# Weight quantizer of a two-layer mixture kernel: the rounding constant from ScalarE's Square instead of VectorE's masked exponent

## The chip, the cores and the metric

The kernel runs on one core of a Trainium2 chip. The metric is the device time of one launch in microseconds, the median of three runs. A profile is one further execution of the same program; its times come from that execution.

## The reference

The reference is a two-layer transformer body on x of 4 x 512 tokens of width 512. Only the first two of its four sublayers matter here:

1. x = x + tanh(g) * E(layernorm(x)), where E is a three-matrix expert (Wg, Wu and Wd are all `ctx_2048[e]`), and a token's expert e of four follows from its id. Tokens are sorted by expert into 19 slots of 128 rows.
2. x = x + tanh(g) * FFN(layernorm(x)), a SiLU-gated feed-forward net with 2048 hidden units whose activations and weights are rounded block by block. For a weight w the rounding is:

```
amax  = max |w| over a block of 32
scale = 2 ** (floor(log2(amax)) - 2)
v     = w / scale
step  = 2 ** (max(floor(log2|v|), 0) - 1)
q     = clip(round_half_to_even(v / step) * step, -6, 6) * scale
```

Layer 1 (attention over ctx, then a routed mixture of 64 experts) follows in the same kernel and is not touched.

## The kernel before, in words

All stages are in one program with one hand-written instruction stream for each engine, joined by semaphores. Stage 1 (about 15 to 213 us of the profile) does sublayer 1 and, beside it, quantizes and transposes the weights of sublayer 2, which stage 2 needs complete.

Sublayer 1 runs over SLOTS = 19 slots j. For a slot, GpSimd (POOL) gathers 128 rows by an indirect DMA (`gather`, L585), VectorE (DVE) takes mean and variance (`measure`, L904 and L905), POOL turns them into a scale and a bias (`deviation`, L592 to L594), ScalarE (ACT) normalises (`normal_h`, L1632), TensorE (PE) transposes (`turn_h`, L1283), ACT copies out of PSUM (`ht`, L1637), PE multiplies by the expert's matrix (`z`, L1294), ACT takes SiLU (`silu`, L1642), DVE the product (`product`, L910), PE transposes it (`turn_a`, L1303), ACT copies (`at`, L1647), PE multiplies again (`y`, L1310), ACT scales and copies (`y`, L1652), and POOL adds the rows into x_sum in DRAM by an indirect DMA (`scatter`, L616).

The weights are 16 tiles n of 128 x 1536 (512 columns each of gate, up and down). For a tile, SP loads it (L488 to L490), DVE takes the maximum of each block of 32 (`top`, L865), and makes the block's power of two and its inverse (`scales`, L871 and L874), and POOL multiplies the tile by the inverse into wy (`normal`, L600). Then DVE rounds by adding and subtracting a large constant, in two functions:

- `push` (L876 to L885): masks the exponent bits out of wy's upper half (L880), makes of them the constant ws = max(., 1/4) * 1.5 * 2^22 in bf16 (L883), and adds: wu = ws + wy (L885).
- `pull` (L887 to L895): wc = wu - ws (L890), clamps to +-1.5 (L892), multiplies by the block's power of two into wq (L895).

PE transposes wq in twelve pieces (`turn_w`, L1320) and ACT copies them into the stationary weights (`weights`, L1659 to L1662).

The order of the work is written out by hand. Tiles are paired with slots by TILED: slots with j % 4 != 3 have a tile, so 15 tiles have a slot and tile 15 comes after the last slot (REST). In a slot with tile n the engines do, in this order:

- DVE: scales(n+1), top(n+2), measure(j+4), product(j+1), pull(n), push(n+1); push(0) stands ahead of the loop, before measure(3)
- POOL: normal(n+1), scatter(j-1), deviation(j+3), gather(j+5)
- PE: z(j+1), turn_a(j), turn_h(j+2), turn_w of slot j-1, y(j)
- ACT: silu(j+1), at(j), ht(j+2), weights of slot j-1, y(j), normal_h(j+3)

Ahead of the loop ACT does normal_h(0), ht(0), normal_h(1), issues four DMAs (L1674), then silu(0), ht(1), normal_h(2). Stage 2 begins with SP's loads of x_sum (L508), which wait for the last scatter, and DVE's `enter` (L948), which stands behind the last pull.

Of the kernel before, what the change touches and what calls it, by code (L numbers as in the profile page):

```python
# [8 lines left out]
BF16 = mybir.dt.bfloat16  # L9
# [8 lines left out]
P = 128  # L18
# [17 lines left out]
W_MAGIC = 1.5 * 2.0 ** 22  # L36
W_TOP = 1.5
W_LOW = 0.25
# [58 lines left out]
def build(nc, x, ids, ctx, g_xattn, g_ffn, w_gate, w_up, w_down, gamma, gate_w, bias,  # L97
# [9 lines left out]
    with ExitStack() as st:  # L107
# [52 lines left out]
        def bank(n, m=1):  # L160
# [18 lines left out]
        wmax_ready, wm_ready, winv_ready, wy_ready, we_ready, ws_ready, wu_ready, wc_ready, wtop_ready, wq_ready = (  # L179
            sem(n) for n in ("wmax_ready", "wm_ready", "winv_ready", "wy_ready", "we_ready", "ws_ready", "wu_ready",  # L180
# [13 lines left out]
        we_bits = arena(W3 // 2, I16)  # L194
        ws = arena(W3 // 2, BF16)
# [287 lines left out]
        with nc.Block() as block:  # L483
# [302 lines left out]
            def _(dve):  # L786
# [90 lines left out]
                def push(n):  # L877

                    dve.wait_ge(wy_ready, n + 1)
                    dve.tensor_scalar(we_bits, wy[:, n % 2, :].bitcast(I16)[:, 1::2], EXP_MASK16, None,  # L880
                                      ALU.bitwise_and).then_inc(we_ready, 1)
                    dve.wait_ge(we_ready, n + 1)
                    dve.tensor_scalar(ws, we_bits.bitcast(BF16), W_LOW, W_MAGIC, ALU.max, ALU.mult).then_inc(ws_ready, 1)  # L883
                    dve.wait_ge(ws_ready, n + 1)
                    dve.tensor_tensor(wu, ws, wy[:, n % 2, :], ALU.add).then_inc(wu_ready, 1)  # L885

                def pull(n):  # L887

                    dve.wait_ge(wu_ready, n + 1)
                    dve.tensor_tensor(wc[:, n % 2, :], wu, ws, ALU.subtract).then_inc(wc_ready, 1)  # L890
                    dve.wait_ge(wc_ready, n + 1)
                    dve.tensor_scalar(wc[:, n % 2, :], wc[:, n % 2, :], W_TOP, -W_TOP, ALU.min, ALU.max).then_inc(wtop_ready, 1)  # L892
                    dve.wait_ge(wtop_ready, n + 1)
                    need(dve, wq_turned, n - 1)
                    dve.tensor_tensor(twos(wq[:, n % 2, :]), twos(wc[:, n % 2, :]),  # L895
                                      wm[:, n % 4].unsqueeze(2).to_broadcast([P, NB3, BLK // 2, 2]), ALU.mult).then_inc(wq_ready, 1)
# [21 lines left out]
                push(0)  # L918
                measure(3)
                product(0)  # L920
                for j in range(SLOTS):
                    n = tile_at(j)
                    if j in TILED:
                        scales(n + 1)
                        if n + 2 < NT:
                            top(n + 2)
                    if j + 4 < SLOTS:
                        measure(j + 4)
                    if j + 1 < SLOTS:
                        product(j + 1)  # L930
                    if j in TILED:
                        pull(n)
                        push(n + 1)
                for n in REST:
                    if n + 1 < NT:
                        scales(n + 1)
                    if n + 2 < NT:
                        top(n + 2)
                    pull(n)
                    if n + 1 < NT:  # L940
                        push(n + 1)
# [680 lines left out]
            def _(act):  # L1622
# [30 lines left out]

                def weights(n):
# [4 lines left out]
                    act.activation(WGT[:, :, cols], src[:, 0], ACT.Copy)  # L1659
                    act.activation(WUT[:, :, cols], src[:, 1], ACT.Copy)  # L1660
                    r = n % 4
                    act.activation(WDT[:, 4 * (n // 4):4 * (n // 4) + 4, r * P:(r + 1) * P], src[:, 2], ACT.Copy).then_inc(wq_out, 1)  # L1662
# [14 lines left out]
                normal_h(2)  # L1677
                for j in range(SLOTS):
# [3 lines left out]
                    if j + 2 < SLOTS:  # L1682
                        ht(j + 2)
                    if j - 1 in TILED:
# [199 lines left out]
```

## Time and profile before

| | us |
|---|---|
| median of 3 runs | 1055.89 (1052.69 to 1056.42) |
| time of the profiled execution | 1055.53 |
| span of its profile | 1053.7 |
| PE busy | 960.7 (91%) |
| DVE busy | 656.9 (62%) |
| POOL busy | 638.7 (61%) |
| ACT busy | 398.9 (38%) |

The span runs from the first to the last instruction seen; the time of the execution holds another 1.8 us around it. Busy shares are means over stages with different limits. An engine's stream is in order, so an instruction that waits holds up all that stands behind it on its engine.

### The profile page before, as it was taken

To read this page: it belongs to the slowest core of one execution; us is meant where nothing else is said; L and a number is where in the kernel's file an instruction comes from. 1 tells how busy PE (TensorE), PEld (TensorE's weight loads), DVE (VectorE), ACT (ScalarE), POOL (GpSimd) and SP (SyncE) were. 2 spreads that over 40 slices of the span, in tenths; PEclk is the share of its full clock that TensorE was granted. 3 is DMA by queue.
4 is the path that set the end of the run, shared out by engine and by line. 5 is a ranking of instruction groups with operands and counts; after the bars stand their busy time and mean duration, and the time that the engine had idled before them with its cause. 6 is when DMAs were issued, how large, how long until landed. Compare 5 with 4: busy or idle time off the path is not lost.

```text
span 1053.7 us, 13591 instructions
## 1 busy us (share of the span) xinstructions
PE 960.7 (91%) x4380; PEld 470.5 (45%) x4402; DVE 656.9 (62%) x1208; ACT 398.9 (38%) x801; POOL 638.7 (61%) x562
## 2 busy tenths in 40 slices
PE   4989999659999999799999999999999999999993
PEld 3445554324444444344444445335555555555530
DVE  6679887968888887677777777981222222222221
ACT  4434445324444444466666665332111111111100
POOL 4497887548878887686767671245444554445431
PEclk9989999869999999999999999999999999999996
DMA  7755555240000000240000605078999999999949
GB/s 260 239 121 138 125 127 131 39 160 1 2 1 1 1 2 13 75 163 21 21 21 25 245 1 200 21 260 259 335 335 331 334 339 330 335 334 338 253 54 193
DMA packets 64147, 162.89 MB, mean 155 GB/s; under 512 B 9888, under 2 KB 10032, under 8 KB 63632
## 3 DMA queue, kind: packets, MB, share of 16 engines
q1 hardware_dynamic: 47488, 116.94, 31.9%
q0 software_dynamic: 16464, 40.91, 18.0%
q10 hardware_dynamic: 128, 4.19, 1.2%
q8 instruction: 37, 0.61, 0.2%
q14 instruction: 30, 0.25, 0.1%
HBM read 129.67 MB, written 39.67 MB: 161 GB/s over the span
## 4 chain that ended last, share of the span: by engine, by line
PE 55%; POOL 17%; DVE 14%; issue 8%; ACT 2%; DMA 1%; ACTq 0%; POOLq 0%; DVEq 0%
PE PS L1570 16%; PE PS L1589 8%; PE PS L1414 6%; PE PS L1391 6%; PE PS L1402 6%; POOL ARENA L657 6%; POOL ARENA L663 3%; PE PS L1559 3%; PE PS L364 3%; DVE ARENA L985 2%; POOL XNT L600 2%; DVE ARENA L890 2%; POOL ARENA L652 1%; PE PS L1310 1%; DVE ARENA L1194 1%
## 5 line engine op out<-in xcount | busy, mean ns | idle before, releaser
L707 POOL TENSOR_TENSOR ARENA<-ARENA 128x512 f32<-128x512 f32 x128 | 133.2, 1061 | 54.5 <-DVE ARENA L1020 54.4
L1356 PE MATMUL PS<-SLAB,ARENA 128*128 128x512 bf16 x501 | 119.4, 385 | 13.4 <-DVE ARENA L971 10.8
L753 POOL DMA_INDIRECT out<-ARENA,idx x32 | 45.9, 1436 | 125.3 <-DVE ARENA L1226 116.3
L1836 ACT ACTIVATE ARENA<-PS 96x192 f32<-96x192 f32 x64 | 20.9, 326 | 226.4 <-PE PS L1570 226.4
L1226 DVE COPY ARENA<-PS 96x512 f32<-96x512 f32 x64 | 41.1, 682 | 94.8 <-PE PS L1589 94.8
L1743 ACT ACTIVATE ARENA<-PS,ARENA 128x512 f32<-128x512 f32 x128 | 86.8, 683 | 24.4 <-DVE ARENA L1014 21.2
L1014 DVE TENSOR_REDUCE ARENA<-PS 128x2 f32<-128x1024 f32 x64 | 78.2, 1221 | 8.3 <-PE PS L1391 8.0
L1356 PEld LDWEIGHTS PS<-SLAB,ARENA 128*128 128x128 bf16 x512 | 48.8, 99 | 76.1 <-issue 23.1
L1570 PE MATMUL PS<-SLAB,ARENA 128*96 128x384 f32 x240 | 81.0, 490 | 0.0
L1402 PEld LDWEIGHTS PS<-ident,ARENA 128*128 128x128 f32 x512 | 54.8, 141 | 51.1 <-issue 35.0
L663 POOL TENSOR_TENSOR ARENA<-ARENA 128x1024 bf16<-128x1024 fp8e4 x32 | 61.1, 1909 | 24.3 <-DVE ARENA L985 24.3
L657 POOL TENSOR_TENSOR ARENA<-ARENA 128x1024 f32<-128x1024 f32 x32 | 62.8, 1962 | 21.5 <-DVE ARENA L980 21.5
L1709 ACT ACTIVATE ARENA<-PS 128x512 f32<-128x512 f32 x64 | 38.2, 597 | 99.1 <-PE PS L1356 99.0
L746 POOL DMA_INDIRECT ARENA<-rows,idx x64 | 60.0, 938 | 23.4 <-issue 11.6
L1294 PE MATMUL PS<-CT,ARENA 128*128 x152 | 70.8, 610 | 2.8 <-ACT ARENA L1637 2.8
L1391 PE MATMUL PS<-ARENA 64*128 64x512 f32 x256 | 72.5, 643 | 0.2 <-ACT ARENA L1743 0.2
L1310 PE MATMUL PS<-CT,XNT 128*128 x152 | 70.7, 608 | 2.2 <-ACT XNT L1647 2.1
L1402 PE MATMUL PS<-ident,ARENA 128*128 128x128 f32 x512 | 70.7, 280 | 1.7 <-DVE XNT L1027 1.7
L1214 DVE SCALAR_TENSOR_TENSOR ARENA<-PS,ARENA 96x192 f32<-96x192 f32 x64 | 26.2, 409 | 69.9 <-ACT ARENA L1836 69.9
L1414 PE MATMUL PS<-XNT,CT 128*64 128x512 f32 x256 | 68.2, 616 | 0.0
L600 POOL TENSOR_TENSOR XNT<-XNT,ARENA 128x1536 f32<-128x1536 f32 x16 | 45.6, 2851 | 33.5 <-DVE ARENA L874 33.3
L1375 PE MATMUL PS<-SLAB,ARENA 128*128 128x512 bf16 x245 | 59.9, 385 | 0.9 <-issue 0.3
(265 smaller groups left out, 1841.4 us busy)
## 6 DMA issues: line engine op xcount, KB each, us to landing
SLAB<-in_L_ffn_w_gate SPq DMA_DIRECT2D x30, 384.0 KB, 20.0
SLAB<-in_L_ffn_w_up SPq DMA_DIRECT2D x30, 384.0 KB, 20.0
X<-in_L_ffn_w_down SPq DMA_DIRECT2D x14, 768.0 KB, 22.0
SLAB<-in_L_ffn_w_down SPq DMA_DIRECT2D x10, 768.0 KB, 22.0
CT<-in_L_ffn_w_gate SPq DMA_DIRECT2D x16, 384.0 KB, 20.5
CT<-in_L_ffn_w_up SPq DMA_DIRECT2D x16, 384.0 KB, 20.5
X<-in_ctx SPq DMA_DIRECT2D x4, 1024.0 KB, 8.9
XNT<-in_L_ffn_w_gate SPq DMA_DIRECT2D x16, 256.0 KB, 2.7
```

The source lines that it names most:

```text
L657: pool.tensor_tensor(blocks(iy[:, h, :]), blocks(inter[:, par, h, :]), spread(iinv[:, h, :]), ALU.mult).then_inc(iy_ready, 1)
L663: pool.tensor_tensor(blocks(qi[:, par, h, :]), blocks(ic[:, h, :]), spread(im[:, par, h, :]), ALU.mult).then_inc(iq_ready, 1)
L707: last = pool.tensor_tensor(prob[s % 4][:, h, :], prob[s % 4][:, h, :], rec[:, s % 4, h:h + 1].to_broadcast([P, D]), ALU.mult)
L1014: dve.tensor_reduce(nmax[:, s % 4, :], bank(2 * (s % 2), 2).rearrange("p (h d) -> p h d", h=2), AX.X, ALU.max, negate=True).then_inc(max_r ...
L1310: last = pe.matmul(bank(4 + j % 2), aT[:, j % 2, k * P:(k + 1) * P], CT[:, bass.ds(e, 1), k, :].rearrange("p a s -> p (a s)"), start=(k == ...
L1356: last = pe.matmul(bank(b), QT[:, par, k * P:(k + 1) * P], w[:, k, c * D:(c + 1) * D], start=(k == 0), stop=(k == KD - 1))
L1391: last = pe.matmul(bank(2 * (s % 2) + h), qn[rows_h, i % 2, c * P:(c + 1) * P], keys4[rows_h, i % 4, :], start=True, stop=True)
L1402: last = pe.transpose(bank(4 + h)[:, k * P:(k + 1) * P], prob[s % 4][:, h, k * P:(k + 1) * P], ident[:, :])
L1414: last = pe.matmul(bank(6 + i % 2)[h * DH:h * DH + DH, :], CT[:, b, k, r * P + h * DH:r * P + h * DH + DH], PT[h][i % 2][:, k, :], start=( ...
L1570: last = pe.matmul(bank(2 + e % 2)[0:CAP, 0:2 * F1].rearrange("p (n f) -> p n f", n=2), bT[:, e % 2, k, :], gate_up_of(e)[:, :, k, :], sta ...
L1589: last = pe.matmul(bank(4 + n)[0:CAP, :], hT6[half, t % 2, m, :], down_of(t)[half, m, :], start=(m == 0), stop=(m == 2))
L1743: last = act.activation(prob[s % 4][:, h, :], bank(2 * (s % 2) + h), ACT.Exp, bias=nmax[:, s % 4, h:h + 1], accum_out=esum[:, s % 4, h:h + 1])
```

## The change

The rounding constant of a weight is no longer made from its exponent bits. ACT computes ws = (W_SCALE * wy)^2 in bf16, with W_SCALE^2 = (8/3) * 2^20. DVE adds the constant W_BASE = 1.34375 * 2^20 to it inside three-operand instructions: wu = (ws + W_BASE) + wy in `push`, and wc = (ws + W_BASE) - wu in `pull`. So wc has the opposite sign, which ACT's copies in `weights` undo by a scale of -1. The two one-input instructions L880 and L883 are gone, and so is the semaphore between them; ws has two buffers instead of one.

The streams change so: DVE's push(n) moves from slot n's predecessor to the slot of tile n, directly ahead of pull(n), and push(0) leaves its place ahead of the loop. ACT gets square(0) behind normal_h(2), and square(n+1) in each slot with a tile, behind ht(j+2) and ahead of weights and y(j). square(n) waits for POOL's normal(n), and for pull(n-2)'s first instruction, which frees the buffer. The order of slots and tiles is the same.

```diff
-W_MAGIC = 1.5 * 2.0 ** 22
+W_BASE = 1.34375 * 2.0 ** 20
+W_SCALE = (8.0 / 3.0) ** 0.5 * 2.0 ** 10
 W_TOP = 1.5
-W_LOW = 0.25
...
-        we_bits = arena(W3 // 2, I16)
-        ws = arena(W3 // 2, BF16)
+        ws = arena(W3, BF16).rearrange("p (r d) -> p r d", r=2)
...
                 def push(n):
 
-                    dve.wait_ge(wy_ready, n + 1)
-                    dve.tensor_scalar(we_bits, wy[:, n % 2, :].bitcast(I16)[:, 1::2], EXP_MASK16, None,
-                                      ALU.bitwise_and).then_inc(we_ready, 1)
-                    dve.wait_ge(we_ready, n + 1)
-                    dve.tensor_scalar(ws, we_bits.bitcast(BF16), W_LOW, W_MAGIC, ALU.max, ALU.mult).then_inc(ws_ready, 1)
                     dve.wait_ge(ws_ready, n + 1)
-                    dve.tensor_tensor(wu, ws, wy[:, n % 2, :], ALU.add).then_inc(wu_ready, 1)
+                    dve.scalar_tensor_tensor(out=wu, in0=ws[:, n % 2, :], scalar=W_BASE, in1=wy[:, n % 2, :],
+                                             op0=ALU.add, op1=ALU.add).then_inc(wu_ready, 1)
 
                 def pull(n):
 
                     dve.wait_ge(wu_ready, n + 1)
-                    dve.tensor_tensor(wc[:, n % 2, :], wu, ws, ALU.subtract).then_inc(wc_ready, 1)
+                    dve.scalar_tensor_tensor(out=wc[:, n % 2, :], in0=ws[:, n % 2, :], scalar=W_BASE, in1=wu,
+                                             op0=ALU.add, op1=ALU.subtract).then_inc(wc_ready, 1)
...
                 measure(2)
-                push(0)
                 measure(3)
...
                     if j in TILED:
+                        push(n)
                         pull(n)
-                        push(n + 1)
                 for n in REST:
...
+                    push(n)
                     pull(n)
-                    if n + 1 < NT:
-                        push(n + 1)
...
+                def square(n):
+
+                    act.wait_ge(wy_ready, n + 1)
+                    need(act, wc_ready, n - 1)
+                    act.activation(ws[:, n % 2, :], wy[:, n % 2, :], ACT.Square, scale=W_SCALE).then_inc(ws_ready, 1)
+
                 def weights(n):
...
-                    act.activation(WGT[:, :, cols], src[:, 0], ACT.Copy)
-                    act.activation(WUT[:, :, cols], src[:, 1], ACT.Copy)
+                    act.activation(WGT[:, :, cols], src[:, 0], ACT.Copy, scale=-1.0)
+                    act.activation(WUT[:, :, cols], src[:, 1], ACT.Copy, scale=-1.0)
...
                 normal_h(2)
+                square(0)
                 for j in range(SLOTS):
...
                         ht(j + 2)
+                    if j in TILED:
+                        square(tile_at(j) + 1)
                     if j - 1 in TILED:
                         weights(tile_at(j - 1))
                     y(j)
```

## Rows read from the trace of the kernel before

**Rows 1.** Stretches: busy us (instructions) of PE, PEld, DVE, ACT, POOL; PEclk, DMA share, GB/s.
```profile
30.00:60.00 30.00, 22.65 (x80) 11.38 (x78) 21.07 (x28) 10.55 (x17) 15.95 (x15) 0.96 0.68 218
60.00:90.00 30.00, 29.46 (x115) 16.27 (x116) 23.44 (x31) 14.87 (x28) 24.23 (x19) 0.93 0.47 115
...
131.30:166.00 34.70, 33.68 (x137) 17.67 (x135) 30.88 (x40) 16.64 (x30) 29.66 (x23) 1.00 0.54 128
```

**Rows 2.** PE's waits, 60 to 185 us: us in total, times, longest.
```profile
PE PS L1283 <- ACT ARENA L1632: 7.3, 4, 5.1
```

**Rows 3.** Instructions in order of time around 50 to 60 us: start, duration, what.
```profile
49.32 0.19 DVE L874 TENSOR_SCALAR ARENA<-ARENA 128x48 int16<-128x48 int16 x1
...
52.52 3.23 POOL L616 DMA_INDIRECT x_sum<-ARENA  x1 [0.17 <-issue]
...
57.82 1.43 POOL L594 TENSOR_SCALAR ARENA<-ARENA 128x1 f32<-128x1 f32 x1
...
60.15 1.11 PE L1283 MATMUL PS<-ident,ARENA 128*128 128x128 f32 x4 [5.09 <-ACT ARENA L1632]
```

**Rows 4.** DVE's groups of instructions, 0 to 260 us: busy us, mean ns.
```profile
L890 DVE TENSOR_TENSOR ARENA<-ARENA 128x1536 bf16<-128x1536 f32 x16 | 28.8, 1802 | 0.0
L885 DVE TENSOR_TENSOR ARENA<-ARENA,XNT 128x1536 f32<-128x1536 bf16 x16 | 28.1, 1758 | 0.6
...
L895 DVE TENSOR_TENSOR ARENA<-ARENA 128x1536 bf16<-128x1536 bf16 x16 | 15.3, 958 | 0.6
L880 DVE TENSOR_SCALAR ARENA<-XNT 128x1536 int16<-128x1536 int16 x16 | 15.3, 953 | 0.9 <-POOL XNT L600 0.9
...
L883 DVE TENSOR_SCALAR ARENA<-ARENA 128x1536 bf16<-128x1536 bf16 x16 | 9.0, 560 | 0.6
```

**Rows 5.** DVE's groups over the whole span, the three-operand form with SBUF sources.
```profile
L1175 DVE SCALAR_TENSOR_TENSOR CT<-ARENA 128x512 f32<-128x512 f32 x2 | 1.4, 682 | 0.0
```

**Rows 6.** ACT's groups over the whole span.
```profile
L1709 ACT ACTIVATE ARENA<-PS 128x512 f32<-128x512 f32 x64 | 38.2, 597 | 99.1 <-PE PS L1356 99.0
...
L1714 ACT ACTIVATE ARENA<-PS 128x1024 bf16<-128x1024 bf16 x32 | 32.7, 1021 | 6.1 <-PE PS L1367 5.9
...
L1632 ACT ACTIVATE ARENA<-ARENA 128x512 f32<-128x512 f32 x19 | 15.4, 809 | 27.1 <-POOL ARENA L594 27.1
```

**Rows 7.** Instructions in order of time, 27 to 33 us.
```profile
27.57 1.39 POOL L594 TENSOR_SCALAR ARENA<-ARENA 128x1 f32<-128x1 f32 x1
...
31.27 0.27 POOL L594 TENSOR_SCALAR ARENA<-ARENA 128x1 f32<-128x1 f32 x1
...
31.45 0.60 PE L1283 MATMUL PS<-ident,ARENA 128*128 128x128 f32 x4
...
31.55 1.28 ACT L1642 ACT_TABLE_LOAD   x1 [1.74 <-issue]
```

**Rows 8.** ACT in order of time, the next load of a table.
```profile
424.53 1.28 ACT L1743 ACT_TABLE_LOAD   x1
427.55 0.69 ACT L1743 ACTIVATE ARENA<-PS,ARENA 128x512 f32<-128x512 f32 x1 [1.73 <-DVE ARENA L1014]
```

**Rows 9.** Instructions in order of time, 191 to 214 us.
```profile
191.41 2.75 POOL L600 TENSOR_TENSOR XNT<-XNT,ARENA 128x1536 f32<-128x1536 f32 x1 [9.08 <-DVE ARENA L874]
...
197.53 2.13 POOL L616 DMA_INDIRECT x_sum<-ARENA  x1 [0.30 <-ACT ARENA L1652]
...
201.06 4.19 POOL L600 TENSOR_TENSOR XNT<-XNT,ARENA 128x1536 f32<-128x1536 f32 x1 [1.40 <-DVE ARENA L874]
202.07 0.69 ACT L1652 ACTIVATE ARENA<-PS,tgate 128x512 f32<-128x512 f32 x1 [2.19 <-PE PS L1310]
...
205.41 2.21 POOL L616 DMA_INDIRECT x_sum<-ARENA  x1 [0.16 <-issue]
...
210.63 12.94 SPq L508 DMA_DIRECT2D X<-x_sum  x16
...
213.59 0.69 DVE L948 BATCH_NORM_STATS2 ARENA<-X 128x6 f32<-128x512 f32 x1
```

More of the change, by code:

```diff
@@ L178, in build @@
         y_stored = [sem(f"y_stored{r}") for r in range(2)]
-        wmax_ready, wm_ready, winv_ready, wy_ready, we_ready, ws_ready, wu_ready, wc_ready, wtop_ready, wq_ready = (
-            sem(n) for n in ("wmax_ready", "wm_ready", "winv_ready", "wy_ready", "we_ready", "ws_ready", "wu_ready",
+        wmax_ready, wm_ready, winv_ready, wy_ready, ws_ready, wu_ready, wc_ready, wtop_ready, wq_ready = (
+            sem(n) for n in ("wmax_ready", "wm_ready", "winv_ready", "wy_ready", "ws_ready", "wu_ready",
                              "wc_ready", "wtop_ready", "wq_ready"))
@@ L1658, in weights @@
                     cols = slice(n * P, n * P + P)
-                    act.activation(WGT[:, :, cols], src[:, 0], ACT.Copy)
-                    act.activation(WUT[:, :, cols], src[:, 1], ACT.Copy)
+                    act.activation(WGT[:, :, cols], src[:, 0], ACT.Copy, scale=-1.0)
+                    act.activation(WUT[:, :, cols], src[:, 1], ACT.Copy, scale=-1.0)
                     r = n % 4
-                    act.activation(WDT[:, 4 * (n // 4):4 * (n // 4) + 4, r * P:(r + 1) * P], src[:, 2], ACT.Copy).then_inc(wq_out, 1)
+                    act.activation(WDT[:, 4 * (n // 4):4 * (n // 4) + 4, r * P:(r + 1) * P], src[:, 2], ACT.Copy, scale=-1.0).then_inc(wq_out, 1)
                 act.wait_ge(g_in, 48)
```

## The prediction
> **What bounds the kernel now.** I first read the page's slices: PE is busy nine tenths and more nearly everywhere, except in the first slices and about 200 to 230 us. The change touches only stage 1, so I read that stage by stretches. From 131.3 to 166.0 us (four slots, three of them with a tile) PE is busy 33.68 of 34.70 us and DVE 30.88 [rows 1]. So PE bounds the steady part, with DVE close behind. From 30 to 60 us PE works only 22.65 of 30 us [rows 1]. PE's own waits from 60 to 185 us are few: 7.3 us for ACT's normal_h, of which 5.1 us is one wait and the other three make 2.2 us [rows 2]. The long one is turn_h(4), which starts at 60.15 us. Followed back, it waits for POOL's deviation(4), whose last instruction starts at 57.82; that stands behind scatter(0) at 52.52 (3.23 us); that behind normal(2), which waits for DVE's scales(2), whose second instruction starts at 49.32 [rows 3]. So in this place DVE's queue, in front of scales, decides. After the wait PE's granted clock is lower: 0.93 as a mean over 60 to 90 us, where it is 1.00 later [rows 1].
>
> At the end of the stage two things meet: DVE's own tail, behind which `enter` starts at 213.59, and the load of x_sum, issued at 210.63, which waits for scatter(18) of 205.41 [rows 9]. Stage 2 and all behind it start from there, so a shift there should carry to the end of the kernel.
>
> **The change part by part.**
>
> *DVE's instructions.* Removed: L880 and L883, 0.953 + 0.560 = 1.51 us for a tile [rows 4]. Two two-input instructions of 1.76 and 1.80 us become three-operand ones. The trace has that form with SBUF sources at 512 columns: 0.682 us [rows 5]. Between both ends: if a second operation is free, 1.76 us as now; if it takes a second pass, twice that, 3.5 us. At 512 columns the form isn't doubled, so I scale it as one pass: 1.77 us each. DVE thus saves about 1.5 us a tile, 24 us in all of DVE's time, most of it covered by PE.
>
> The Trainium skill (Vector Engine (DVE) Microarchitecture Reference, Points that are easy to get wrong) says that this form loses half its throughput when both SBUF sources are not bf16. Here one source is bf16, and the row above, with both sources f32, took 0.682 us, so I hold the trace against it; were it so, both would take some 3.4 us. It is rival B.
>
> *ACT's Square.* Not in the trace. Its ends: the slope between 512 and 1024 columns is (1021 - 597) / 512 = 0.83 ns a column, so from 597 ns one gets 1.45 us for 1536 columns; from the SBUF row with two per-partition operands, 809 ns, 1.66 us [rows 6]. It has neither, so I take 1.48. Sixteen of them are 24 us of an engine that is busy 16.64 of 34.70 us [rows 1]; 3 x 1.48 = 4.4 us more leaves it below two thirds. The scale of -1 in `weights` costs nothing: L1709 carries an immediate scale and takes 597 ns [rows 6].
>
> *Start, part 1.* Today push(0) runs beside deviation(1) on POOL, whose last instruction took 1.39 us, against 0.27 for the same one of deviation(2) [rows 7]. With push(0) gone from there all three go at their free speed; I estimate that deviation(1) then ends about 2.1 us earlier (1.1 of it from the last one), near 26.8. Behind it on ACT stand normal_h(1), the four DMA issues and then the load of SiLU's table at 31.55, which starts as soon as the queue reaches it: the later load at 424.53 ran well before its ACTIVATE's wait ended [rows 7, 8]. So the load moves to about 29.4 and ends before z(0) does (PE's next instruction, turn_h(1), starts at 31.45 [rows 7]). silu(0) then starts 1.25 us earlier, at 31.6 instead of 31.55 + 1.28, and everything PE does behind it too: **1.25 us**. gather(4) also moves up 2.1 us, ahead of the DMAs that slow it.
>
> *Start, part 2, the wait at 60.* In slot 0 DVE did pull(0) and push(1), now push(0) and pull(0): 1.5 us less, and 1.3 to 2 us sooner if gather(4) lands sooner. So scales(2) comes near 46 to 47.5 instead of 49.1, and scatter(0) then runs beside push(1), a one-pass instruction, instead of the clamp, the product and the mask, beside which it took 3.23 us [rows 3]. I have deviation(4) end at 53.6 to 55.5 instead of 57.82 + 1.43 = 59.25, turn_h(4) starts 0.9 us later, at 54.5 to 56.4, and PE is ready for it at 60.15 - 5.09 - 1.25 = 53.8. Of the 5.1 us some 1.9 stay: **3.2 us**. If that short a wait leaves the clock up, 7 hundredths of 30 us return [rows 1]: **2.1 us**; if not, nothing. The other three waits, 2.2 us, are for the same ACT line and have the same form (POOL late behind DVE's scales); DVE is then 1.5 us a tile ahead, so I count **1.9** of them [rows 2].
>
> *What speaks against it: the order in ACT's queue.* square(n+1) waits for POOL's normal(n+1), and weights and y(j) stand behind it. In steady slots normal ends about when ht does, so nothing is late. At the end it is: normal(15) stands behind scatter(17), which ran from 197.53 to 199.66, and then meets push(14) on DVE, which I have at 198.3 to 200.1. normal(15) took 4.19 us beside L890, which has two SBUF inputs, and normal(14) 2.75 us [rows 9]; so I let it start when push(14) ends. On PE's line of before that gives normal(15) to 202.9, square(15) to 204.4, weights(13) to 205.9, y(18) at 205.9 instead of 202.07, scatter(18) at 206.7 instead of 205.41, about half a microsecond shorter. So the loads of x_sum start 0.8 us later than 210.63. DVE's tail goes on from 202.9 with pull(14), push(15) and pull(15): 2 x (1.77 + 0.56 + 0.96) + 1.77 = 8.4 us (the clamp has L883's form) [rows 4], so to about 211.4, 2 us before today's end, and then waits for the load. The end of stage 1 thus gains nothing and loses **0.8 us**.
>
> The Trainium skill (SBUF — State Buffer, SBUF: two separate sides) says that a DVE instruction with two SBUF inputs excludes a GpSimd one that reads SBUF, for the whole instruction. The 4.19 us above agree. By this rule the new forms, both with two SBUF inputs, stand as much in POOL's way as the two removed, which alone would bring POOL nothing; by a free POOL deviation(4) would end near 52.3 and turn_h(4) would not wait.
>
> *Sum.* 1.25 + 3.2 + 2.1 + 1.9 - 0.8 = 7.65, which I round to 7.7 us. The profiled execution's 1055.53 becomes 1047.8; it lies 0.4 below the median 1055.89, so I forecast 1048.0.
>
> **The rivals.**
>
> A. *Most of the gain is lost in queues* (the wait at 60 only shrinks by the 1.5 us that DVE saves, since gather(4) still lands late and POOL's small instructions now run beside three one-pass or two-input ones; the clock still falls; y(18) is later still). For it: POOL is busy 29.66 of 34.70 us [rows 1] and fragile. Against: DVE's queue is the last wait in Rows 3. Then 1.25 + 1.5 + 0.9 - 1.2 = 2.5: 1053.4.
>
> B. *The three-operand form takes two passes*, slower. DVE has 34.7 - 30.9 = 3.8 us to spare in a period of four slots [rows 1] and gains 4.5 by the two removed, so 8.3 us for six instructions: it decides from 1.77 + 1.4 = 3.2 us each. At 3.45 us they cost 6 x 1.68 = 10.1 us more, 1.8 over that, 7 us in four periods; DVE's tail of four tiles, exposed at the end, grows by 4 x (3.36 - 1.5) = 7.4; the wait at 60 grows by some 3; the first 1.25 us are still gained. That is +16 on 1055.9: 1071 to 1072. Against it: [rows 5].
>
> C. *Square needs another table than SiLU.* Each tile then has two loads of 1.28 us [rows 8] on ACT, 16.64 + 4.4 + 7.7 = 28.7 us busy of 34.7, with ACT's answers to PE in between: I put 1 us on each of 15 slots and 5 on the start, 1075. Against: Copy, Identity and SiLU share a table already, as the row at 31.55 [rows 7] is the last load before 424.53 [rows 8].
>
> D. *The change does more*: turn_h(4) finds everything ready, and y(18) isn't late: 1.25 + 5.1 + 2.1 + 2.2 = 10.6, so 1045.2.
>
> **How the numbers follow.** My forecast has 0.50 (its own range 1046 to 1051), D 0.14, A 0.26, B 0.05, C 0.03, and 0.02 for other slowdowns. The range for 8 in 10 reaches from D's time with a little below to A's with a little above: 1044.0 to 1055.5. A difference of under 0.5% (5.3 us, so between 1050.6 and 1061.2) is about what can't be told from no change. Faster holds D, and nine tenths of the forecast's own case: 0.14 + 0.46 = 0.60. Same holds the rest of it and A: 0.31. Slower: B, C and some: 0.09.
>
> **What would show it.** L880 and L883 gone; the two new ones near 1.77 us at 128x1536, not 3.4. Square near 1.48 us and no further table load before 400 us. silu(0) about 1.2 us earlier. PE's wait for normal_h in slot 2 under 2.5 us instead of 5.1, its clock 1.00 from 60 to 90 us. Steady periods of 34.0 to 34.2 instead of 34.7 us. y(18) on ACT behind square(15) and weights(13), and `enter` started not by DVE's tail but by the load of x_sum, about 7.7 us earlier than 213.59. I am wrong if PE waits somewhere new in the slots, above all for ht, at or silu behind a square, or if stage 2 gives back what stage 1 gained.

## The result and the profile after

The change made the kernel slower: 1064.98 us as a median of 7 runs (1060.50 to 1066.44), against 1055.89 us before (1049.78 to 1056.43), a ratio of 1.0094 with a 95% interval of [1.0074, 1.0113]. The profiled execution took 1061.29 us, with a span of 1059.6 us against 1053.7. I had forecast 1048.0 and at most 1055.5.

The milestones say where the loss arises. Start of ACT's silu(j) and y(18), and of DVE's `enter`, read from the timelines of both kernels, in us:

| | silu(0) | silu(2) | silu(3) | silu(4) | silu(12) | silu(18) | y(18) | `enter` |
|---|---|---|---|---|---|---|---|---|
| before | 32.8 | 46.2 | 60.0 | 70.5 | 139.8 | 191.5 | 202.1 | 213.6 |
| after | 31.3 | 44.7 | 62.6 | 72.2 | 145.2 | 198.9 | 212.8 | 222.3 |
| after - before | -1.5 | -1.5 | +2.6 | +1.7 | +5.4 | +7.4 | +10.7 | +8.7 |

So there are four pieces: 1.5 us gained at the start, 3.2 lost up to silu(4), 5.7 lost in the steady slots, 1.3 lost from silu(18) to `enter`. Behind `enter` the profiled run has 837.3 us against 840.1. The profiles of the experiments below have 838.2 to 840.5 there whatever was changed, so I don't read that as an effect, and the 8.7 us at `enter` are near the 9.1 between the medians. How far the pieces can be trusted one by one is said under the experiments: that of the steady slots is firm, that up to silu(4) is not.

The instructions themselves came out as worked out. DVE's and ACT's groups of the changed kernel, 0 to 260 us (out<-in, shape, count | busy us, mean ns | idle before them, what ended it):

```profile
L885 DVE SCALAR_TENSOR_TENSOR ARENA<-ARENA 128x1536 bf16<-128x1536 bf16 x16 | 30.6, 1911 | 0.5
L879 DVE SCALAR_TENSOR_TENSOR ARENA<-ARENA,XNT 128x1536 f32<-128x1536 bf16 x16 | 28.1, 1756 | 0.0
...
L900 DVE BATCH_NORM_STATS2 ARENA<-ARENA 128x6 f32<-128x512 f32 x19 | 13.1, 688 | 25.1 <-DMA ARENA<-in_x,ARENA 23.9 <-issue 1.2
...
L1652 ACT ACTIVATE ARENA<-XNT 128x1536 bf16<-128x1536 f32 x16 | 23.8, 1488 | 17.4 <-POOL XNT L599 17.3
```

L879 answers to the sum and L885 to the difference of [rows 4]: the same 1756 ns and a mean of 1911. One of the 16 took 4.20 us and the rest 1.76. Square (L1652) takes 1488 ns. The busy time of DVE fell from 656.9 to 634.0 us, that of ACT rose from 398.9 to 421.0. But PE, which bounds the stage, got less work done in its stretches. Columns as in [rows 1]; the third row stands beside 28.98 us of PE and a clock of 1.00 in the kernel before:

```profile
30.00:60.00 30.00, 22.75 (x71) 11.68 (x70) 16.31 (x20) 13.89 (x19) 11.53 (x9) 0.83 0.54 185
60.00:90.00 30.00, 28.68 (x116) 15.09 (x115) 21.29 (x28) 16.51 (x26) 27.64 (x21) 1.00 0.53 121
...
120.00:150.00 30.00, 27.58 (x110) 14.77 (x109) 21.94 (x30) 16.31 (x26) 27.64 (x21) 0.94 0.51 117
```

From 30 to 60 us the clock is 0.83 where it was 0.96 [rows 1]; POOL is busy 11.53 us instead of 15.95, so something holds it up. From 60 to 90 us POOL is busy 27.64 us instead of 24.23, though the program gives it no instruction more (562 in both kernels). PE's waits of the changed kernel, 60 to 206 us:

```profile
PE PS L1277 <- ACT ARENA L1626: 6.7, 6, 1.9
PE PS L1304 <- ACT XNT L1641: 1.7, 5, 0.4
PE PS L1314 <- DVE ARENA L891: 1.1, 1, 1.1
```

The 5.1 us wait of [rows 2] is gone and six short ones stand there, 6.7 us for normal_h (L1626), where the kernel before had three with 2.2. These 4.5 us more are most of the 5.7 lost in the steady slots. What is left is about the clock's part: PE's busy time from silu(4) to silu(18) is 119.25 us instead of 117.33, and its granted clock, 1.00 all through these slots before, is 0.66 from 145 to 150 us, directly behind a wait of 1.91 us:

```profile
145.40 0.84 PE L1277 MATMUL PS<-ident,ARENA 128*128 128x128 f32 x4 [1.91 <-ACT ARENA L1626]
146.02 1.49 PE L1314 MATMUL PS<-ident_b,ARENA 128*128 128x128 bf16 x12
```

The same twelve matmuls of turn_w take 0.83 us where the clock is up.

**The start.** The changed kernel in order of time. deviation(1), three undisturbed instructions of which L593 is the last, ends at 26.7, and the table load is at 29.70 instead of 31.55 [rows 7]:

```profile
25.41 0.33 SPq L487 DMA_DIRECT2D XNT<-in_L_ffn_w_gate  x1
...
26.26 0.43 SPq L489 DMA_DIRECT2D XNT<-in_L_ffn_w_down  x1
26.46 0.27 POOL L593 TENSOR_SCALAR ARENA<-ARENA 128x1 f32<-128x1 f32 x1
...
26.77 2.90 ACTq L1674 DMA_DIRECT2D x_sum<-in_x  x4
...
29.70 1.28 ACT L1636 ACT_TABLE_LOAD   x1 [2.12 <-issue]
...
31.34 0.60 ACT L1636 ACTIVATE ARENA<-PS 128x512 f32<-128x512 f32 x1 [0.36 <-PE PS L1288]
...
44.41 1.75 DVE L864 TENSOR_REDUCE ARENA<-XNT 128x48 f32<-128x1536 f32 x1 [11.41 <-DMA XNT<-in_L_ffn_w_down]
...
46.89 0.65 DVE L906 TENSOR_TENSOR XNT<-ARENA,PS 128x512 f32<-128x512 f32 x1
...
47.60 1.12 PE L1297 MATMUL PS<-ident,XNT 128*128 128x128 f32 x4 [2.96 <-DVE XNT L906]
...
52.75 0.19 DVE L873 TENSOR_SCALAR ARENA<-ARENA 128x48 int16<-128x48 int16 x1
```

The gain brought its own loss. ACT's four copies of x to x_sum stand right behind normal_h(1), so they too moved up, from 29.00 to 26.77. There they start 0.1 us after SP has issued the load of weight tile 2 (from 25.41 to 26.69, the end of the last line of that load). In the kernel before they came 1.4 us after it, and top(2) ran at 34.42 without a wait. Now top(2) waits 11.41 us for that load, to 44.41, and DVE works in order: product(1) comes behind it at 46.89, PE waits 2.96 us for it, and scales(2), which I had at 46 to 47.5, comes at 52.75.

**The steady slots.** One slot of the changed kernel in order of time:

```profile
92.16 1.75 DVE L879 SCALAR_TENSOR_TENSOR ARENA<-ARENA,XNT 128x1536 f32<-128x1536 bf16 x1
...
93.11 0.89 POOL L591 TENSOR_SCALAR ARENA<-ARENA 128x1 f32<-128x1 f32 x1
...
93.95 1.76 DVE L885 SCALAR_TENSOR_TENSOR ARENA<-ARENA 128x1536 bf16<-128x1536 bf16 x1
...
94.09 2.25 POOL L592 TENSOR_TENSOR ARENA<-ARENA,neg_half 128x1 f32<-128x1 f32 x1
95.75 0.56 DVE L888 TENSOR_SCALAR ARENA<-ARENA 128x1536 bf16<-128x1536 bf16 x1
96.34 0.96 DVE L891 TENSOR_TENSOR ARENA<-ARENA 128x1536 bf16<-128x1536 bf16 x1
96.45 1.02 POOL L593 TENSOR_SCALAR ARENA<-ARENA 128x1 f32<-128x1 f32 x1
```

The three instructions of a deviation, one element a partition each, took 0.23, 0.57 and 0.27 us when nothing stood beside them (at 28 us). Here L591 ends 0.09 us after L879 does, L592 starts with L885 and ends 0.63 after it, and L593 ends 0.17 after L891: 0.89 + 2.25 + 1.02 = 4.2 us instead of 1.1. push and pull now stand back to back, 3.5 us of two-input instructions; before, the clamp, the product by the scale, the mask and L883 lay between the difference and the next sum. From 0 to 260 us:

```profile
L592 POOL TENSOR_TENSOR ARENA<-ARENA,neg_half 128x1 f32<-128x1 f32 x19 | 26.2, 1378 | 1.6
...
L591 POOL TENSOR_SCALAR ARENA<-ARENA 128x1 f32<-128x1 f32 x19 | 12.8, 674 | 2.6 <-DVE ARENA L901 1.2
L593 POOL TENSOR_SCALAR ARENA<-ARENA 128x1 f32<-128x1 f32 x19 | 12.1, 635 | 2.0
```

Together 51.1 us against 40.9 before (8.9 + 13.7 + 18.3). Behind each deviation stands POOL's next gather, for which DVE waits at L900 (23.9 us from 28 to 206 us, 15.9 before), and ACT's normal_h, for which PE waits. The Trainium skill (SBUF — State Buffer, SBUF: two separate sides) has a two-input DVE instruction shut GpSimd's SBUF reads out for its whole length; by that rule L592 can do its 0.57 us only behind 95.71, and it ends at 96.34, so the trace agrees.

What shuts POOL out is not the two-input instructions alone. In the kernel before, L594 ends 0.05 us after the mask, which has one input, and at the end of the stage the clamp, one input too and 0.56 us elsewhere, takes 3.00 us: it ends 0.42 us behind normal(15), which ran from 201.06 for 4.19 us [rows 9].

```profile
93.05 1.37 POOL L594 TENSOR_SCALAR ARENA<-ARENA 128x1 f32<-128x1 f32 x1
93.42 0.95 DVE L880 TENSOR_SCALAR ARENA<-XNT 128x1536 int16<-128x1536 int16 x1
...
202.67 3.00 DVE L892 TENSOR_SCALAR ARENA<-ARENA 128x1536 bf16<-128x1536 bf16 x1
```

So the old order had collisions of its own (deviations of 2.1 to 3.4 us in nearly all slots with a tile); the new one makes them longer.

**The tail.** The changed kernel:

```profile
206.19 3.75 POOL L599 TENSOR_TENSOR XNT<-XNT,ARENA 128x1536 f32<-128x1536 f32 x1
...
207.35 4.20 DVE L885 SCALAR_TENSOR_TENSOR ARENA<-ARENA 128x1536 bf16<-128x1536 bf16 x1
209.97 1.48 ACT L1652 ACTIVATE ARENA<-XNT 128x1536 bf16<-128x1536 f32 x1 [4.89 <-POOL XNT L599]
...
212.79 0.70 ACT L1646 ACTIVATE ARENA<-PS,tgate 128x512 f32<-128x512 f32 x1
...
219.44 3.74 SPq L507 DMA_DIRECT2D X<-x_sum  x6
...
222.33 0.69 DVE L942 BATCH_NORM_STATS2 ARENA<-X 128x6 f32<-128x512 f32 x1 [3.89 <-DMA X<-x_sum]
```

y(18) stands behind square(15) and weights(13), as forecast, and `enter` waits for the load and no longer for DVE [rows 9]. But y(18) is 10.7 us late, 3.3 of it arisen here.

### The profile page after: what moved, and what is told of

It reads as the page before. It is cut to its first block, busy times and chain, and to the rows that moved or that the text cites. A ratio compares the mean times of both kernels' runs of the same rounds, so it can differ in the third digit from the quotient of the medians.

```text
span 1059.6 us, 13611 instructions
## 1 busy us (share of the span) xinstructions
PE 965.1 (91%) x4402; PEld 472.0 (45%) x4402; DVE 634.0 (60%) x1176; ACT 421.0 (40%) x817; POOL 645.0 (61%) x562
## 3 DMA queue, kind: packets, MB, share of 16 engines
q10 hardware_dynamic: 128, 4.19, 1.1%
## 4 chain that ended last, share of the span: by engine, by line
PE 53%; POOL 22%; DVE 9%; issue 7%; DMA 4%; ACT 1%; SPq 1%; POOLq 0%; DVEq 0%; ACTq 0%
PE PS L1564 16%; PE PS L1583 8%; PE PS L1385 6%; PE PS L1396 6%; PE PS L1408 6%; POOL ARENA L656 6%; POOL XNT L599 3%; POOL ARENA L662 3%; PE PS L1553 3%; DMA XNT<-in_L_ffn_w_down 3%; PE PS L363 3%; POOL x_sum L615 2%; POOL ARENA L592 2%; DVE ARENA L979 2%; POOL ARENA L651 1%
## 5 line engine op out<-in xcount | busy, mean ns | idle before, releaser
L1746 ACT ACTIVATE ARENA<-PS,ARENA 128x512 f32<-128x512 f32 x128 | 86.8, 683 | 23.1 <-DVE ARENA L1008 19.8
L1396 PEld LDWEIGHTS PS<-ident,ARENA 128*128 128x128 f32 x512 | 54.8, 141 | 51.1 <-issue 36.6
L745 POOL DMA_INDIRECT ARENA<-rows,idx x64 | 60.2, 940 | 23.3 <-issue 10.7
L1288 PE MATMUL PS<-CT,ARENA 128*128 x152 | 70.5, 608 | 1.6 <-ACT ARENA L1631 1.6
```

The lines of the kernel that those rows point to most:

```text
L1396: last = pe.transpose(bank(4 + h)[:, k * P:(k + 1) * P], prob[s % 4][:, h, k * P:(k + 1) * P], ident[:, :])
L1746: last = act.activation(prob[s % 4][:, h, :], bank(2 * (s % 2) + h), ACT.Exp, bias=nmax[:, s % 4, h:h + 1], accum_out=esum[:, s % 4, h:h + 1])
```

## The experiments

All were timed in five rounds beside the kernel before, whose median lay between 1053.5 and 1054.7 us there; so compare by the ratio. Each says from which kernel it starts: "before" or "changed". A number with silu or `enter` is its start less that of the kernel before, from the profiled run.

| experiment | median us | ratio to before, 95% | silu(4) | silu(18) | `enter` |
|---|---|---|---|---|---|
| changed | 1064.98 | 1.0094 [1.0074, 1.0113] | +1.7 | +7.4 | +8.7 |
| 1 copies late | 1058.74 | 1.0038 [1.0025, 1.0051] | -2.3 | +1.2 | +2.4 |
| 2 before, push moved | 1074.98 | 1.0192 [1.0177, 1.0207] | +4.1 | +17.5 | +21.2 |
| 3 changed, old order | 1062.63 | 1.0062 [1.0043, 1.0082] | +2.1 | +5.8 | +7.1 |
| 4 deviation first | 1053.23 | 0.9979 [0.9967, 0.9991] | +0.8 | -2.0 | -0.7 |
| 5 last square behind y | 1058.20 | 1.0051 [1.0032, 1.0071] | +0.3 | +4.2 | +1.9 |
| 6 before, copies early | 1057.02 | 1.0038 [1.0021, 1.0054] | +2.2 | +2.0 | +2.0 |
| 7 before, deviation first | 1052.18 | 0.9984 [0.9971, 0.9996] | -6.5 | -3.5 | -3.5 |
| 8 changed with 1, 4 and 5 | 1047.20 | 0.9946 [0.9927, 0.9966] | -2.3 | -5.2 | -7.2 |
| 9 before, Square added | 1056.68 | 1.0031 [1.0016, 1.0045] | -2.8 | -2.8 | +1.0 |
| 10 before, form only | 1054.01 | 1.0003 [0.9990, 1.0017] | -2.7 | -2.8 | -2.8 |
| 11 before with 1 and 4 | 1051.90 | 0.9982 [0.9967, 0.9997] | -5.3 | -3.3 | -3.3 |
| 12 as 8, copies on SP | 1044.66 | 0.9913 [0.9898, 0.9928] | -6.0 | -8.0 | -9.9 |
| 13 changed, top between | 1071.43 | 1.0154 [1.0134, 1.0175] | -0.3 | +12.5 | +16.4 |
| 14 as 12, top between | 1059.92 | 1.0042 [1.0024, 1.0059] | -4.3 | +2.1 | +4.9 |
| 15 changed, top behind product | 1065.19 | 1.0101 [1.0079, 1.0123] | -1.4 | +7.5 | +10.5 |

Experiments 9 and 10 show how far one profiled run is to be trusted: neither changes anything that could speed the start, 10 has the time of the kernel before, and yet both profiles are 2.7 us ahead at silu(4). The wait at 60 us is 5.1 us long in the profile of before and 2.8 in theirs. So an offset under 3 us from one profile decides nothing here; the ratios do. For the pieces of the loss this means: from silu(2) to silu(4) the changed kernel loses 3.2 us against the profile of before and 6.0 against that of 10, while from silu(4) to silu(18) the profiles of before, 9 and 10 agree within 0.2 us (121.1, 121.0, 120.9).

### What the copies cost (1, 6, 12)

```diff
 (1)             normal_h(1)
-                for b in range(B): act.dma_start(x_sum...)
                 silu(0)
                 ht(1)
+                for b in range(B): act.dma_start(x_sum...)
 (6) before: the same four copies ahead of normal_h(1) instead of behind it
```

> The changed kernel, but ACT issues its four copies of x into x_sum behind silu(0) and ht(1) instead of ahead of them, so well after the load of weight tile 2. Theory 1 (the copies, issued at 26.8 instead of 29.0 us, now overtake that load, and top(2) waits 11.4 us for it): top(2) waits under 1 us, product(1) comes near 37 to 40 us, PE's waits in slots 1 and 2 (3.0 and 3.1 us) go, and stage 2 starts some 5 us earlier than in the changed kernel; time about 1059 to 1061. Rival (the load is slow by the mass of traffic, in whatever order): top(2) still waits 5 us or more, and the time stays at 1064 to 1066.

> The kernel before, with one edit: ACT issues its four copies of x ahead of normal_h(1), at about 25.6 us instead of 29.0. Theory 1 (the time at which the copies are issued against the load of weight tile 2 decides): top(2), which waits for nothing in the kernel before, waits some 10 us, silu(3) and silu(4) come 2 to 4 us later than in the kernel before, and the time is 1057 to 1060. Rival (that load is slow in the changed kernel for another reason): top(2) is on time, and the time stays within 1 us of 1055 or gains the 1.3 us of an earlier table load.

In 1, top(2) runs at 32.53 without a wait and silu(3) is 7.1 us ahead of before's. The ratio falls by 0.0056, some 6 us. But the copies, now at 31.40, meet the next load:

```profile
31.40 0.61 ACTq L1676 DMA_DIRECT2D x_sum<-in_x  x1
32.05 1.88 ACTq L1676 DMA_DIRECT2D x_sum<-in_x  x3
...
35.49 0.33 SPq L487 DMA_DIRECT2D XNT<-in_L_ffn_w_gate  x1
...
49.45 1.75 DVE L864 TENSOR_REDUCE ARENA<-XNT 128x48 f32<-128x1536 f32 x1 [6.70 <-DMA XNT<-in_L_ffn_w_down]
```

Experiment 6 gives the kernel before a like collision (copies from 24.38, the load from 25.40), and it costs 4 us there (0.0038), with nothing else moved:

```profile
43.05 1.75 DVE L865 TENSOR_REDUCE ARENA<-XNT 128x48 f32<-128x1536 f32 x1 [9.56 <-DMA XNT<-in_L_ffn_w_down]
```

Experiment 12 tells time from queue: the copies start at the very moment that was fatal in the changed kernel, but in SP's queue.

```diff
 (12) SP:        load_w(tile_at(j) + 2)
+                if j == 0:
+                    for b in range(B): sp.dma_start(x_sum...)
```

> The fastest kernel so far (deviation first, last Square behind y(18), copies late) with the four copies issued by SyncE directly behind its load of weight tile 2 instead of by ScalarE behind silu(0). Theory (copies that stand in the same queue behind the load no longer slow it, and tile 3's load comes after most of their traffic): top(2) waits under 3 us, top(3) under 3 us, PE's wait for turn_w near 57 us shrinks, 1043 to 1046. Rival (what counts is when the copies run, not their queue: issued right behind the load they share the DMA engines with it, and top(2) waits 8 us or more): 1049 to 1053.

```profile
26.18 0.43 SPq L489 DMA_DIRECT2D XNT<-in_L_ffn_w_down  x1
26.65 2.74 SPq L504 DMA_DIRECT2D x_sum<-in_x  x4
...
33.26 1.74 DVE L867 TENSOR_REDUCE ARENA<-XNT 128x48 f32<-128x1536 f32 x1
...
48.06 1.75 DVE L867 TENSOR_REDUCE ARENA<-XNT 128x48 f32<-128x1536 f32 x1
```

Neither top(2) nor top(3) waits. In experiment 4, with the copies in ACT's queue from 26.72, top(2) waits 10.98 us. So what delays the load is that the copies run in another queue beside it; behind it in its own queue they do no harm. The rival, that only the moment counts, falls. Otherwise 12 is 8, below, and the ratio falls from 0.9946 to 0.9913, some 3.5 us. This is the fastest kernel of the study, 1044.66 us.

### What the pair of two-input instructions costs (2, 3, 4, 7, 13, 15)

```diff
 (4), (7) POOL, slot j:
+                deviation(j + 3)
                 normal(tile_at(j) + 1)
                 scatter(j - 1)
-                deviation(j + 3)
 (2) before: push(n) directly ahead of pull(n), and none ahead of the loop
 (3) changed: pull(n), push(n + 1), and push(0) ahead of the loop; square(0) ahead of silu(0)
 (13) changed:   push(n)
+                top(n + 2)
                 pull(n)
 (15) changed:   product(j + 1)
+                top(n + 2)
                 push(n)
```

> The kernel before, with its own arithmetic on DVE and no Square, but with push(n) directly ahead of pull(n) as in the change, and no push(0) ahead of the loop. Theory 2 (the place of push costs: POOL's deviation then meets DVE's two two-input instructions in a row, and all DVE work of a tile lies in one piece): deviation's instructions grow as in the changed kernel, PE waits more for normal_h, time 1059 to 1064. Rival (what costs is the three-operand form or ACT's Square, not the place): the steady slots stay at 34.7 us a period; only the first slots differ, since deviation(1) is freed and the copies start early as in the changed kernel, so 1056 to 1059.

> The changed kernel with DVE's old order: push(n+1) behind pull(n); push(0) stands between measure(3) and product(0), and square(0) ahead of silu(0) so that it is ready. Theory 2 (the place of push): the waits of PE for normal_h in the steady slots fall back to 2 us or less, and silu 4 to 17 gain nothing or lose under 1 us against the kernel before, instead of losing 5.7; time 5 us under the changed kernel, near 1059. Rival (Square or the form): the loss between silu 4 and silu 17 stays at 5 us or more.

> The changed kernel, but on POOL deviation(j+3) stands first in its slot, ahead of normal and scatter, so beside DVE's top and measure instead of the two three-operand instructions. Theory 2: deviation's three instructions take about 0.24, 0.57 and 0.27 us, PE's waits for normal_h in the steady slots go (6.7 us now), and the loss between silu 4 and silu 17 (5.7 us now) turns into a gain of 0 to 2 us; time about 1056 to 1059. Rival (the steady loss comes from ACT's queue, where silu and normal_h stand behind a Square that waits for normal): normal and so Square come later, and the waits stay or grow; 1064 or more.

> The kernel before, with POOL's deviation(j+3) first in its slot, as in the earlier run of the changed kernel with that edit (1053.2 us). Theory 2 (in the changed kernel POOL's small instructions meet the two three-operand instructions; in the kernel before they cost PE only 2.2 us of waits): deviation's sum falls to 1.1 to 1.5 us in most slots, PE's three short waits go, the time is 1052 to 1054, so the change's own part under a free POOL is about nothing. Rival (the reordering itself is worth 10 us in either kernel): 1045 or less.

Experiment 2 puts the kernel before in the new order, and it loses 20 us (1074.98, where 1059 to 1064 was expected); from slot 1 on the three instructions of a deviation take 3.1 to 5.0 us in slots with a tile, and PE waits for normal_h eight times:

```profile
PE PS L1281 <- ACT ARENA L1630: 11.8, 8, 2.1
```

Not all of the 20 us are the pair's: with push(0) gone the copies come early here too, and top(2) waits 9.29 us. But 13.4 of them arise from silu(4) to silu(18). So the order is the dear part, and the rest of the change gives about half of the 20 us back in the changed kernel. But the old order alone doesn't cure the change: 3 still loses 3.7 us from silu(4) to silu(18), where the theory had under 1 and the rival 5 or more, and takes 1062.63 us instead of about 1059. Its trace shows why: without the mask and L883 the product by the scale (L891) and the next push stand back to back, and L593 is shut out in its turn:

```profile
104.68 0.96 DVE L891 TENSOR_TENSOR ARENA<-ARENA 128x1536 bf16<-128x1536 bf16 x1
105.18 2.18 POOL L593 TENSOR_SCALAR ARENA<-ARENA 128x1 f32<-128x1 f32 x1
105.56 1.75 DVE L879 SCALAR_TENSOR_TENSOR ARENA<-ARENA,XNT 128x1536 f32<-128x1536 bf16 x1
```

Experiment 4 leaves DVE as it is and moves POOL's deviation ahead of normal. The ratio falls from 1.0094 to 0.9979, some 12 us and 3 us more than expected; from silu(4) to silu(18) the slots now gain 2.8 us instead of losing 5.7, and PE has no wait for normal_h left. In 7 the same move gives the kernel before 1.7 us. But the move does two things at once: it takes deviation away from the pair, and it brings it ahead of normal and scatter. In 4 the deviations still take 4.0 to 4.5 us in four slots, where 1.1 was expected, and in 7 they take 45.1 us in all, more than the 40.9 before, and yet PE's waits for normal_h are gone in both. So the earlier place in POOL's queue works by itself in 7 and has its part in the 12 us of 4; how large that part is, no run shows.

> The changed kernel with top(n+2), which has one input, between push(n) and pull(n) instead of behind scales(n+1). Theory (two long two-input instructions back to back shut POOL's deviation out, and top(2) ahead of product(1) passes the late load on to PE): L592's mean falls from 1.38 to under 1 us, PE's waits for normal_h fall from 6.7 to under 2 us, PE's wait for product(1) goes, and the time is 1050 to 1056. Rival (any two-input instruction beside it slows the deviation as much, adjacent or not): deviation sums of 4 to 5 us stay in the slots with a tile and the time is 1059 or more.

> The changed kernel with top(n+2) behind product(j+1) but ahead of push(n) and pull(n), which stay back to back. Theory: PE's wait of 3 us for product(1) near 47 us goes, since product(1) no longer stands behind the late tile 2; the deviations keep their sums of 4 to 5 us and the steady loss from silu(4) to silu(18) stays near 4 to 6 us: 1057 to 1062. Rival (the place of top is what matters, not the pair): as fast as with top between the pair, 1050 to 1056.

Experiment 13 parts the pair on DVE with a one-input instruction and leaves POOL's order alone. Of its theory the first link holds: L592's mean falls from 1378 to 643 ns. PE's waits for normal_h fall from 6.7 to 4.3 us, not under 2.

```profile
L592 POOL TENSOR_TENSOR ARENA<-ARENA,neg_half 128x1 f32<-128x1 f32 x19 | 12.2, 643 | 1.6
```

The time does not: 1071.43 instead of 1050 to 1056. PE's waits, 28 to 206 us, show why:

```profile
PE PS L1314 <- DVE ARENA L891: 12.8, 5, 5.4
PE PS L1277 <- ACT ARENA L1626: 4.3, 3, 1.4
```

I had counted what top holds up ahead of the product, not what it holds up behind the sum. turn_w (L1314) waits for the last instruction of pull, which now comes 1.75 us later in each tile; it waited 4.2 us in the changed kernel. 15 missed its 1057 to 1062 for the same reason: product(1) is on time and silu(4) 1.4 us ahead, but turn_w waits 11.7 us in all and takes it back. The deviations of 15 were expected to keep their 4 to 5 us, and they fell to 1.1 to 2.4. That makes it the cleanest run for the second link, since nothing was moved on POOL: with short deviations PE's waits for normal_h are nearly gone. Its waits, 28 to 206 us:

```profile
PE PS L1314 <- DVE ARENA L891: 11.7, 5, 4.7
...
PE PS L1277 <- ACT ARENA L1626: 0.9, 3, 0.3
```

So DVE's part can't be loosened at no price: what parts the pair or stands ahead of it is paid at turn_w.

### The tail, the form and the Square alone (5, 9, 10)

```diff
 (5) the square of slot 18:   y(j)
+                             square(15)
 (9) before: act.activation(spare, wy[:, n % 2, :], ACT.Square) at the change's places
 (10) before: scalar_tensor_tensor with a scalar of 0.0 for L885 and L890
```

> The changed kernel, but in the last slot alone square(15) stands behind y(18) on ACT instead of ahead of weights(13) and y(18). Theory 3 (at the end of stage 1 that Square, which waits for normal(15), holds up y(18), so scatter(18) and the loads of x_sum): y(18) comes 4 us earlier against y(17), 5.6 us behind it as in the kernel before instead of 8.9, and enter 1 to 3 us earlier against silu(18); time 1062 to 1064. Rival (DVE's tail ends the stage anyway, and push(15) now gets its square later): enter keeps its 1.3 us behind silu(18) or loses more; 1065.

> The kernel before with the Square of the change added on ScalarE at the change's places (square(0) behind normal_h(2), square(n+1) ahead of weights), written to a buffer of its own that nobody reads; VectorE's work and order stay as they were, and POOL's product waits for the Square of two tiles earlier. Theory (the loss comes from POOL's deviation between two long VectorE instructions and from the copies on top of weight tile 2, neither of which is made here): silu(0) and top(2) as before, silu(18) within 1.5 us of before's, only the tail longer, since y(18) stands behind square(15): enter 1 to 3 us later, 1056 to 1059 beside 1055. Rival (the Square delays ScalarE's answers to PE in every slot): silu(18) 4 us or more late and 1060 or more.

> The kernel before with its sum and its difference in the three-operand form with a scalar of 0.0; same values, same order, mask and second step stay. Theory (the form takes one pass, 1.76 and 1.80 us as the two-operand form): 1054 to 1056.5 beside 1055, VectorE's busy time the same within 1 us. Rival (the form shuts POOL out more or longer than the two-operand form with the same two inputs): the deviations of the slots sum to over 3.5 us and the time is 1058 or more.

In 5 y(18) no longer waits for normal(15) (206.82 instead of 212.79), and from silu(18) to `enter` there are 19.8 us against 23.4 with the square ahead of it and 22.1 before. The ratio falls by 0.0043, 4.5 us, which with its interval of some 3 us either way agrees with the 3.6 of the tail; the profiles differ by 3.2 us already at silu(18), though the program is the same up to there, so I count 3.6. Both are more than the 1 to 3 us expected, and the time, 1058.20, lies under the 1062 to 1064. In 9 the Square alone costs 3.3 us (0.0031): none in the slots, but 6.1 us between silu(18) and y(18), of which 3.8 are left at `enter`. 10 shows the form at no price, 1.0003.

### What the change is worth without the collisions (8, 11, 14)

> The changed kernel with the three mends together: copies issued behind ht(1), deviation first in its slot, and the last Square behind y(18). Theories 1 to 3 as separate causes: enter comes near 208 to 210 us (213.6 in the kernel before, 222.3 in the changed one), time 1047 to 1050, under both kernels. Rival (the causes overlap, since PE's wait moves from one to the next): no better than the best of them alone, 1052 to 1054.

> The kernel before with POOL's deviation first in each slot and ScalarE's four copies behind silu(0) and ht(1): the counterpart of the fastest kernel so far (1047.2 us) without the change's arithmetic. Theory (with the collisions gone the arithmetic of the change is worth the 1.5 us a tile that it takes off VectorE, where VectorE decides, so a few us): 1050 to 1053, that is 3 to 6 us above 1047.2. Rival (the arithmetic is worth nothing, all of the gain is the two moves): 1046 to 1048.5. Rival 2 (late copies harm the kernel before, whose copies did not collide): 1054 or more.

> The fastest kernel so far (1044.7 us: deviation first, copies on SyncE behind the load of tile 2, last Square behind y(18)) with top(n+2) between push(n) and pull(n). Theory (measure and product come 1.75 us earlier in each slot with a tile, and POOL's product is less in the way of the pair, but pull comes 1.75 us later, while PE's turn_w already waits for it 10 us in all): 1042 to 1047, so no clear gain. Rival (the gap frees POOL and the waits for turn_w go as well): 1040 or less.

The three repairs together give 1047.20 us, 5.7 us under the kernel before by the ratio, 0.9946. The same moves of deviation and copies in the kernel before give 1051.90. So beside the two moves the change is worth 0.9946 / 0.9982, 3.8 us, with some 2.6 either way; the last square behind y(18) isn't among 11's edits, since the kernel before has none. This is the price of the whole change, the order of push, the form and the Square included: 8 and 11 differ in all of them, and no run has the arithmetic by itself. Nor is 8 free of collisions: its deviations still take 3.6 to 4.5 us in four slots. What remains on PE in 8, 28 to 206 us, is DVE's chain:

```profile
PE PS L1314 <- DVE ARENA L891: 11.7, 4, 3.9
```

14 missed its 1042 to 1047 widely: it lost 15 us (1059.92 against 1044.66). From silu(4) to silu(18) turn_w waits 6.1 us in it and 0.4 in 12, and these slots take 8.3 us longer; another 4.8 us come between silu(18) and `enter`. So this chain must not be lengthened, though the waits of turn_w account for only a part of the 15 us.

## Why the prediction was wrong

- *DVE's instructions and ACT's Square: right.* 1.756 us for the sum and 1.76 for the difference where nothing disturbs it, forecast 1.77; Square 1.488, forecast 1.48; no further table load. Experiment 10 prices the form at nothing. Rivals B and C fall.
- *Start, part 1: right*, 1.5 us forecast as 1.25, in all its links: deviation(1) free at 26.7 (forecast 26.8), the table load at 29.70 (29.4), silu(0) at 31.3 (31.6). What this step left out is the four copies that it names itself as standing between normal_h(1) and the table load. I had counted them as a delay of the load of the table and not asked what they meet when they come 2.2 us earlier.
- *Start, part 2: the step that failed first.* The prediction gave 3.2 us for the wait at 60 and 2.1 for the clock. It put scales(2) at 46 to 47.5; it came at 52.75, since top(2) ahead of product(1) waited 11.41 us for tile 2. The 5.1 us wait at 60 did go, but two waits of 3 us stand for it at 47.6 and 52.7, with the lower clock from 47 on: 0.83 over 30 to 60 us instead of 0.96. Forecast -5.3 us; measured +3.2 from silu(2) to silu(4), or +6.0 against the profile of experiment 10, which has a shorter wait at 60. Experiment 1 (some 6 us back) and 6 (4 us lost in the kernel before) show it as the copies'.
- *The other three waits: the wrong sign.* Forecast -1.9 us, measured +5.7. The working took DVE's 1.5 us a tile as POOL's gain too. I had quoted the rule that two-input instructions shut POOL out and weighed it for normal, whose 2.8 us stretch at most by half, and for the number of such instructions, which didn't change. I did not weigh it for deviation, whose 1.1 us grow to 4.2, nor ask where the instructions now stand: it is adjacency that changed. Experiment 2 shows the order's price, 13 and 15 that the deviations shorten once they meet the pair less, and 15 that PE's waits for normal_h then go; 4, which also moves deviation forward on POOL, has the steady slots gain 2.8 us, a little more than I had counted.
- *The order in ACT's queue: the mechanism right, the size wrong.* -0.8 forecast, 1.3 from silu(18) to `enter` measured, and 3.6 us come back in 5. I had used the DVE tail as a floor that today sets the end; once the load sets it, y(18)'s delay counts nearly in full.
- Of the rivals none describes it. A had the fragile POOL but let the gain go at worst to 2.5 us. That POOL's small instructions could be slower than before was named there and given no number of its own. The trace of before had the sign for a rival on the slower side: its deviations already took 2.1 to 3.4 us in nearly all slots with a tile, against 1.1 in the others.

The repairs do not add up: alone they are worth 6, 12 and 3.6 us, together 15.6 (1.0094 to 0.9946). What each leaves in place takes part of the others' gain. How much of the slots' loss falls to the gather's later issue and how much to normal_h was not tried apart.

## What to carry to other kernels

Where a step moves earlier, list the DMAs that its engine issues behind it, and look at what each of them will run beside; a bulk copy in another queue delays a load that the next step needs, and the cheap cure is to put it behind that load in the same queue. Where an edit brings long two-input DVE instructions together, look at POOL's smallest instructions in those slots, not at its longest, since a 0.6 us one can take 2.3. And an instruction that stands between two others of an in-order queue has two prices, what it holds up if it stands first and what it holds up if it stands last.

## What was not expected of the hardware

- A POOL instruction on one element a partition took 2.25 us beside a 1.76 us DVE instruction with two SBUF inputs, 0.57 alone. The exclusion also runs the other way: L885 took 4.20 us beside normal(15), and an L879 that met a normal took 3.08 in experiment 13; even the one-input clamp took 3.00 instead of 0.56 beside normal(15) in the kernel before.
- Four DMAs of one copy, issued 0.1 us after a tile's load in another queue, kept that load from landing until 44.4 us; in the same queue behind it, it had landed by 33.3.
- The wait at 60 us is 5.1 us in the profile of before and 2.8 in those of 9 and 10, whose edits give no reason for it. Experiment 5 and the changed kernel, the same program up to the last slot, lie 3.2 us apart at silu(18).
